# A GRU recurrence with a weight quantiser beside it: pieces of six blocks instead of seven, and the eight blocks left over quantised in chunks 2 to 6 of layer 0

## What is computed

```
h = scan(GRU cell, cond, x)                    # 32 sequential steps, batch 64, width 256
x = x + attention0(h)                          # 16 heads of 128, causal, q and k normalised
x = x + ffn0(conv0(x, cond) + b)               # 8-bit rows, ternary weights, silu(gate) * up, RMS norm
x = x + attention1(cond_block(x, cond))
x = x + ffn1(conv1(x, cond))                   # weights w_fc, w_proj through mse_quant_dequant

def mse_quant_dequant(w):                      # blocks of 64 along the input dimension, int5
    base = max(max|w| in block, 1e-8) / 15
    for s in linspace(0.4, 1.0, 16):           # keep the scale with the least squared error
        deq = clip(round(w / (base * s)), -15, 15) * base * s
        err = sum((deq - w) ** 2)
    return clip(round(w / best), -15, 15) * best
```

## Time and profile before

| | us |
|---|---|
| median of 3 runs | 1393.39 (1392.47 to 1393.52) |
| profiled execution, its own time | 1392.67 |
| its span | 1390.9 |
| busy: PE, DVE, ACT, POOL | 1296.4, 1134.4, 783.6, 134.8 |

### The profile page before, as it was taken

The page is one execution under the profiler, slowest core; times in us unless marked ns, Lnnn a source line. Parts: engine busy times, 40 slices in busy tenths (PEclk is TensorE's granted clock), DMA queues, the critical chain, the costliest instruction groups (busy, mean ns, idle before and its releaser), DMA issues.

```text
span 1390.9 us, 25071 instructions
## 1 busy us (share of the span) xinstructions
PE 1296.4 (93%) x9490; PEld 928.4 (67%) x9490; DVE 1134.4 (82%) x2903; ACT 783.6 (56%) x1486; POOL 134.8 (10%) x152
## 2 busy tenths in 40 slices
PE   5999999999999999999999848898999999999988
PEld 2444444578778787888877535576777778686867
DVE  4799999789988678686969799578788888878775
ACT  3999998865546565655555544534353534445213
POOL 0000000101020101011011100000111111110100
PEclk9999999999999999999999979898999999999999
DMA  9332332531111120202122310000000000000000
GB/s 380 115 76 65 72 100 64 159 119 35 35 39 47 31 60 19 77 1 77 29 99 82 125 38 1 24 16 16 1 24 1 24 1 24 8 8 9 8 1 23
DMA packets 26533, 74.18 MB, mean 53 GB/s; under 512 B 3992, under 2 KB 5156, under 8 KB 25136
## 3 DMA queue, kind: packets, MB, share of 16 engines
q1 hardware_dynamic: 25840, 71.62, 16.5%
q10 hardware_dynamic: 576, 0.98, 0.2%
HBM read 49.52 MB, written 23.07 MB: 52 GB/s over the span
## 4 chain that ended last, share of the span: by engine, by line
PE 65%; DVE 28%; ACT 4%; issue 2%; DMA 1%; SPq 0%; DVEq 0%; ACTq 0%
PE psum L616 14%; PE psum L966 8%; PE psum L725 7%; PE psum L937 7%; DVE ffn_mem L1944 4%; DVE work L1827 4%; PE psum L664 4%; PE psum L980 3%; DVE work L1958 3%; PE psum L1005 3%; PE psum L629 2%; PE psum L883 2%; PE psum L674 2%; PE psum L960 1%; PE psum L650 1%
## 5 line engine op out<-in xcount | busy, mean ns | idle before, releaser
L616 PE MATMUL psum<-h_all,w_big 128*128 128x256 f32 x1024 | 242.5, 385 | 1.0 <-ACT work L1269 1.0
L616 PEld LDWEIGHTS psum<-h_all,w_big 128*128 128x128 f32 x1024 | 189.0, 191 | 41.1 <-issue 15.3
L1827 DVE SCALAR_TENSOR_TENSOR work<-work,taps 128x248 f32<-128x248 f32 (+30 forms) x558 | 149.5, 347 | 0.0
L570 PE MATMUL psum<-w_big,h_all 128*64 128x512 f32 x512 | 124.2, 607 | 0.0
L937 PE MATMUL psum<-work,w_big 128*128 128x256 f32 x512 | 119.8, 381 | 0.5 <-DVE gru_mem L2377 0.5
L725 PE MATMUL psum<-w_big,gru_mem 128*128 128x256 f32 x512 | 113.6, 379 | 0.5 <-ACT gru_mem L1311 0.5
L966 PE MATMUL psum<-w_big 128*128 128x256 f32 x448 | 107.3, 391 | 0.0
L725 PEld LDWEIGHTS psum<-w_big,gru_mem 128*128 128x128 f32 x512 | 96.9, 190 | 14.7 <-ACT gru_mem L1311 0.6
L937 PEld LDWEIGHTS psum<-work,w_big 128*128 128x128 f32 x512 | 95.5, 190 | 15.7 <-DVE gru_mem L2377 3.3
L966 PEld LDWEIGHTS psum<-w_big 128*128 128x128 f32 x448 | 85.1, 194 | 19.5 <-issue 7.7
L2375 DVE TENSOR_TENSOR gru_mem<-psum,trig 128x256 f32<-128x256 f32 x128 | 53.8, 420 | 44.2 <-PE psum L937 41.2
(11 more groups left out here) (325 smaller groups left out, 2578.5 us busy)
## 6 DMA issues: line engine op xcount, KB each, us to landing
value_rows<-w_emb SPq DMA_DIRECT2D x128, 128.0 KB, 2.3
work<-value_rows SPq DMA_DIRECT2D x16, 1024.0 KB, 5.8
w_big<-in_Wq SPq DMA_DIRECT2D x2, 2048.0 KB, 16.6
w_big<-in_Wo SPq DMA_DIRECT2D x2, 2048.0 KB, 20.9
out<-w_big SPq DMA_DIRECT2D x15, 256.0 KB, 2.0
x_res<-out SPq DMA_DIRECT2D x15, 256.0 KB, 2.7
w_big<-in_Wv SPq DMA_DIRECT2D x1, 2048.0 KB, 17.4
w_big<-in_Wk SPq DMA_DIRECT2D x1, 2048.0 KB, 23.1
```

The lines of the kernel that those rows point to most:

```text
L570: mm = pe.matmul(bank(4 + n)[j * B:(j + 1) * B, :], h_all[:, k, :, 2 * pair + j], w_big[:, 2, k * H * HD + n * 512:k * H * HD + (n + 1) * ...
L616: mm = pe.matmul(bank(n % 2)[:, o * TA:(o + 1) * TA], w_big[:, s, k * H * HD + at:k * H * HD + at + HD], h_all[:, k, bass.ds(i * BA, BA), ...
L1827: ins = dve.scalar_tensor_tensor(dst[:, :, lag:], src[:, :, :T - lag], tap, dst[:, :, lag:], ALU.mult, ALU.add)
```

## The change

The pieces shrink from seven blocks to six: `PB = 6`, `PC` = 384 columns, still eight pieces and 32 groups. 16 blocks are then left over, in two halves of `RB = 8`. The first half is the `rest` of before, in its place. The second half, `last` (512 columns from `LAST_AT`), isn't loaded at the start but after chunk 0, into the part of `w_emb` from which PE takes the last piece in layer 1, so that it is neither stored nor loaded again. Its search runs on DVE: `last_begin` (chunk 2) and `last_errors` (chunks 3 to 6) stand between the row maximum and the wait for POOL's root in `quantise_hidden(c - 1, 0)`; `last_group` (chunks 2 to 5) and `last_out` (chunk 6) stand at the end of the chunk, behind `quantise_y`. `last_out` is `rest_out` on `last`, with the product by the scale, which POOL makes for the rest, on DVE at its end. ACT squares (`last_squares`, chunks 3 to 6) behind `hidden_squares(c - 1, 0)`. SP waits in the last chunk for the last sum before it loads W_qkv, and PE waits for the end of `last_out` before it turns the weights.

```diff
-PB = 7
+PB = 6
-RB = NBLK - PIECES * PB
+RB = (NBLK - PIECES * PB) // 2
+LAST_AT = REST_AT + RC
+        last = w_emb[:, 2 * D:2 * D + RC]
+        last_abs = w_big[:, 2, 2560:2560 + RC]
+        last_tmp = w_big[:, 2, 0:GROUP * RC].rearrange("p (j n) -> p j n", j=GROUP)
@@ sync
-            sp.dma_start(w5[:, PC:], io["w5"][:, PC:]).then_inc(w5_in, 16)
+            sp.dma_start(w5[:, PC:LAST_AT], io["w5"][:, PC:LAST_AT]).then_inc(w5_in, 16)
             def last_chunk(i):
+                sp.wait_ge(rest_sum.sem, 2 * NG)
-                for n in range(PIECES):
+                for n in range(PIECES - 1):
                     sp.dma_start(w5_back[n], w5_dram[:, n * 512:(n + 1) * 512]).then_inc(w5_again, 16)
             chunk(0, False, False)
+            sp.wait_ge(film_sum.sem, 1)
+            sp.dma_start(last, io["w5"][:, LAST_AT:]).then_inc(w5_in, 16)
             chunk(1, False, True)
@@ tensor
-                    pe.wait_ge(w5_again, 16 * PIECES)
+                    pe.wait_ge(w5_again, 16 * (PIECES - 1))
+                    pe.wait_ge(rest_done.sem, 2)
@@ scalar
+            def last_squares(n):
+                act.wait_ge(rest_set.sem, NG + n + 2)
+                rest_sq.raised_by(act.activation(last_tmp, last_tmp, ACT.Square))
                 if tail:
                     hidden_squares(c - 1, 0)
+                    if i > 2:
+                        last_squares(i - 3)
@@ vector
+            def last_begin():
+                dve.wait_ge(w5_in, 32)
+                link(dve.tensor_reduce(rest_amax, blocks(last), AX.X, ALU.max, apply_absolute_value=True))
+                link(dve.tensor_scalar(rest_base, rest_amax, 1e-8, None, ALU.max))
+                link(dve.tensor_scalar(rest_base, rest_base, 1.0 / QMAX, None, ALU.mult))
+                link(dve.reciprocal(rest_inv, rest_base))
+                link(dve.tensor_tensor(blocks(last), blocks(last), per_block(rest_inv), ALU.mult))
+                link(dve.scalar_tensor_tensor(last_abs, last, -1.0, last, ALU.mult, ALU.max))
+            def last_group(g):
+                if g:
+                    dve.wait_ge(rest_sum.sem, NG + g)
+                for j in range(GROUP):
+                    ins = dve.tensor_scalar(last_tmp[:, j, :], last_abs, float(1.0 / SHRINKS[g * GROUP + j]), MAGIC,
+                                            ALU.mult, ALU.add)
+                link(ins)
+                link(dve.tensor_scalar(last_tmp, last_tmp, MAGIC + QMAX, MAGIC, ALU.min, ALU.subtract))
+                for j in range(GROUP):
+                    ins = dve.scalar_tensor_tensor(last_tmp[:, j, :], last_abs, -float(1.0 / SHRINKS[g * GROUP + j]),
+                                                   last_tmp[:, j, :], ALU.mult, ALU.add)
+                rest_set.raised_by(ins)
+            def last_errors(g):
+                dve.wait_ge(rest_sq.sem, NG + g + 1)
+                rest_sum.raised_by(dve.tensor_reduce(rest_err[:, g * GROUP:(g + 1) * GROUP, :].rearrange("p s b -> p (s b)"),
+                                                     blocks(last_tmp.rearrange("p j n -> p (j n)")), AX.X, ALU.add))
...
-            def quantise_hidden(c, g, flink):
+            def quantise_hidden(c, g, flink, meanwhile=None):
                 flink(dve.tensor_reduce(h_max, hid_w, AX.X, ALU.max, apply_absolute_value=True))
+                if meanwhile:
+                    meanwhile()
                 dve.wait_ge(hr_on.sem, GA * c + g + 1)
-                    quantise_hidden(c - 1, 0, tail_link)
+                    quantise_hidden(c - 1, 0, tail_link, lambda: last_errors(i - 3) if i > 2 else last_begin())
                     hidden(c - 1, 1, (0,))
+                if tail:
+                    if i - 2 < NG:
+                        last_group(i - 2)
+                    else:
+                        last_out()
```

More of the change, by code:

```diff
@@ L494, in _ @@
             chunk(0, False, False)
+            sp.wait_ge(film_sum.sem, 1)
+            sp.dma_start(last, io["w5"][:, LAST_AT:]).then_inc(w5_in, 16)
             chunk(1, False, True)
             sp.wait_ge(rest_done.sem, 1)
-            sp.dma_start(w5_dram[:, REST_AT:], rest).then_inc(w5_out, 16)
-            with sp.Fori(0, NA - 3) as last:
-                chunk(last + 2, True, True)
+            sp.dma_start(w5_dram[:, REST_AT:LAST_AT], rest).then_inc(w5_out, 16)
+            with sp.Fori(0, NA - 3) as later:
+                chunk(later + 2, True, True)
             last_chunk(NA - 1)
@@ L1717, in _ @@
             pool.wait_ge(in_step.sem, in_step.at(PIECES + 1, 0))
-            rest_based.raised_by(pool.tensor_tensor(blocks(rest), blocks(w5[:, REST_AT:]), per_block(rest_inv), ALU.mult))
+            rest_based.raised_by(pool.tensor_tensor(blocks(rest), blocks(w5[:, REST_AT:LAST_AT]), per_block(rest_inv), ALU.mult))
             times_scale(PIECES - 2)
@@ L1782, in _ @@
             rest_done.raised_by(pool.tensor_tensor(blocks(rest), blocks(rest), per_block(rest_scale), ALU.mult))
-            with pool.Fori(0, NA - 3) as last:
-                chunk(last + 2, True, True)
+            with pool.Fori(0, NA - 3) as later:
+                chunk(later + 2, True, True)
             head_rms(UNITS - 2)
@@ L1895, in slink @@
                     link(ins, in_step, PIECES)
-                slink(dve.tensor_reduce(rest_amax, blocks(w5[:, REST_AT:]), AX.X, ALU.max, apply_absolute_value=True))
+                slink(dve.tensor_reduce(rest_amax, blocks(w5[:, REST_AT:LAST_AT]), AX.X, ALU.max, apply_absolute_value=True))
                 slink(dve.tensor_scalar(rest_base, rest_amax, 1e-8, None, ALU.max))
@@ new lines, in last_errors, with last_out @@
+            def last_errors(g):
+                dve.wait_ge(rest_sq.sem, NG + g + 1)
+                rest_sum.raised_by(dve.tensor_reduce(rest_err[:, g * GROUP:(g + 1) * GROUP, :].rearrange("p s b -> p (s b)"),
+                                                     blocks(last_tmp.rearrange("p j n -> p (j n)")), AX.X, ALU.add))
+            def last_out():
+                dve.wait_ge(rest_sum.sem, 2 * NG)
+                link(dve.tensor_tensor(rest_err, rest_err, shrinks_sq.unsqueeze(2).broadcast_to([P, NS, RB]), ALU.mult))
+                link(dve.tensor_reduce(rest_best, rest_err.rearrange("p s b -> p b s"), AX.X, ALU.min))
+                link(dve.tensor_tensor(rest_pick, rest_err, rest_best.unsqueeze(1).broadcast_to([P, NS, RB]), ALU.is_gt))
+                link(dve.scalar_tensor_tensor(rest_pick, rest_pick, 2.0, shrinks.unsqueeze(2).broadcast_to([P, NS, RB]),
+                                              ALU.mult, ALU.add))
+                link(dve.tensor_reduce(rest_shr, rest_pick.rearrange("p s b -> p b s"), AX.X, ALU.min))
+                link(dve.reciprocal(rest_ishr, rest_shr))
+                link(dve.tensor_tensor(rest_scale, rest_shr, rest_base, ALU.mult))
+                link(dve.tensor_tensor(blocks(last), blocks(last), per_block(rest_ishr), ALU.mult))
+                link(dve.tensor_scalar(last, last, float(QMAX), -float(QMAX), ALU.min, ALU.max))
+                link(dve.tensor_scalar(last, last, MAGIC, MAGIC, ALU.add, ALU.subtract))
+                rest_done.raised_by(dve.tensor_tensor(blocks(last), blocks(last), per_block(rest_scale), ALU.mult))
```

## The result

| | before | after |
|---|---|---|
| median of 4 runs, us | 1393.45 | 1377.07 |
| lowest and highest | 1392.47 to 1393.73 | 1375.23 to 1377.25 |
| profiled execution, its own time | 1392.67 | 1376.97 |
| its span | 1390.9 | 1375.2 |
| busy: PE, DVE, ACT, POOL | 1296.4, 1134.4, 783.6, 134.8 | 1296.0, 1147.1, 775.0, 134.2 |

The changed kernel takes 0.988 of the time (0.986 to 0.990). It is 16.4 us faster in the medians and 15.7 in the spans of the two traces. DVE works 12.7 us more in all and PE the same. The change pays although it adds work: it takes work from where DVE is in the chain and puts more of it where DVE is not.

A forecast was written before the change was run, and what follows sets the result against it. DVE was taken to bound the recurrence and PE layer 0, with PE setting most recurrence steps after the change. Terms -16.3 - 0.3 + 1.6 = -15.0 us gave 1377.7 profiled, 1378.4 us as median (1374.4 to 1382.5).

The forecast's parts named there:

- The recurrence: Last 28 steps: PE's pitch of 6.95 us sets 26 steps, 7.03 and 6.76 the others; 16.3 us saved.
- Rival (a): Recurrence: DVE still sets the steps, at about 6.86 us; 18.7 us saved, kernel 1376.0; chance 0.15.
- The start: Early load: 256 KB less before the constants land saves at most 0.7 us; 0.3 taken.
- After the recurrence: End of the recurrence: DVE ends its quantiser tail sooner but waits for PE's value tiles; nothing gained.
- the stall: Hidden quantiser, chunks 2 to 6: added DVE work delays the third hidden product and so PE; 1.6 us lost.
- the slack of 0.30: Chunks 2 to 6: third hidden product ends at 533.60, PE wants it for its weights at 533.93; 0.30 us spare.
- less what the load overlaps: Chunks 3 to 6: PE's delay of about 0.4 us each, reduced by the load's overlap to 0.34.
- The group fits: End of chunks: a group's 5.22 us fits into 5.69 us of DVE idleness with 0.47 to spare; costs nothing.
- rival (b): Chunks: thinner cover, DVE delays paid whole (3.6 us), groups overrun by 0.4 x 4; 1382.0 us; chance 0.13.
- Rival (d): Chunks: the added 37.3 us of DVE work is not hidden; paid whole 1414.1 us, slower; chance 0.04.
- The rule against it: Chunk 2: two-input DVE products would wait for POOL's power, 1.3 us once; left out of the sum.

The follow-up runs named there:

- the kernel with the work in the chunks alone: Kernel before (seven blocks a piece) plus the last eight blocks' load and search in chunks 2 to 6, done twice: median 1397.76 us, ratio 1.003.
- the doubled group: Changed kernel with each group of four at the end of chunks 2 to 5 computed twice: 1401.09 us, 1.007 of before.

## Why the prediction was right, point by point

1377.07 us against a forecast of 1378.4 (1374.4 to 1382.5), faster as expected. The mechanism is the forecast's; of its terms, some were off in size.

**The recurrence: right, -16.07 for -16.3.** PE's pitch was taken from the single step that PE had set in the kernel before, 6.95 us; 26 steps run at 6.94 to 6.97. Half of the small miss is step 30, 7.16 us for 7.03, the other half the 0.006 by which the 26 steps exceed 6.95; step 31 had 6.75 for 6.76. The prices per column held to 3 ns. Rival (a) was nearer than its 0.15 suggests: DVE stands 0.09 us behind PE.

**The start: the term was mis-sized, -1.19 for -0.3, and for another reason.** The constants land 0.62 us earlier, near the 0.7 that was the bound. DVE timelines of the instruction that waits for them, before and after:

```profile
21.55 0.21 DVE L1993 TENSOR_SCALAR cols<-cols 128x1 f32<-128x1 f32 x1 [4.46 <-DMA shrink_tab<-in_shrinks]
```

```profile
20.93 0.21 DVE L2049 TENSOR_SCALAR cols<-cols 128x1 f32<-128x1 f32 x1 [3.60 <-DMA shrink_tab<-in_shrinks]
```

But the transposition of step 1 starts at 24.01 us instead of 24.19, 0.18 earlier. In the chain after, ACT's scalings of the first group come last there, and no longer the landing:

```profile
18.55 2.14 ACT work L1210 x4
```

In the second trace of the changed kernel this transposition starts at 24.34, so the 0.3 of the forecast can't be told from scatter. The other microsecond of the first pair lies in step 2, and is the clock. Windows of 8 us over step 2: before, after, and the kernel with the work in the chunks alone, whose early load is before's:

```profile
24.00:32.00 8.00, 7.33 (x24) 2.69 (x26) 6.83 (x18) 4.25 (x8) 0.94 (x1) 0.60 1.01 428
```

```profile
23.80:31.80 8.00, 7.30 (x30) 2.86 (x30) 6.63 (x19) 3.93 (x8) 0.83 (x1) 0.79 1.00 426
```

```profile
24.00:32.00 8.00, 6.63 (x26) 2.58 (x28) 6.92 (x19) 4.68 (x9) 0.94 (x1) 0.79 1.02 432
```

At a clock of 0.60 the step, from one transposition to the next, is 9.3 us long, at 0.79 it is 8.3 and 8.1. The third kernel has the early load of before and the clock of after, so the smaller load is not the cause. What else is, stays open; both traces of the kernel before have the long step 2 (9.3 us), all others 8.0 to 8.3.

**After the recurrence: 0 forecast, -0.46 measured.** The argument that DVE's tail brings nothing held. Not seen was that PE's wait for step 31's state shrinks from 2.15 to 1.48 us. Behind the longer one, part of the next 24 products ran at the lower clock (6.94 us for 24; at the 3.72 for 16 of the kernel after it would be 5.58). Windows of 4 us behind it, before and after:

```profile
252.00:256.00 4.00, 4.00 (x12) 2.71 (x9) 2.72 (x6) 4.00 (x7) 0.00 (x0) 0.57 0.50 115
```

```profile
235.00:239.00 4.00, 4.00 (x18) 2.96 (x16) 2.75 (x6) 4.00 (x8) 0.00 (x0) 1.00 0.44 101
```

PE gains 1.4 us there and then waits 0.97 more for ACT's copies, so 0.46 is left. It repeats: both traces of before have 142.77 us in this stretch, the second of after 142.31.

**Chunks 2 to 6: right in place, the stall mis-sized, +0.60 for +1.6.** Timelines of the changed kernel: DVE, PE and PE's weight loads (PEld) in chunk 4, then DVE at the end of chunk 2 (columns as in the earlier trace rows):

```profile
511.62 2.29 DVE L1979 TENSOR_REDUCE v<-w_big 128x32 f32<-128x2048 f32 x1 [0.58 <-ACT w_big L1285]
513.82 0.20 DVE L2189 TENSOR_SCALAR stats<-stats 128x1 f32<-128x1 f32 x1
...
516.03 0.74 DVE L2169 SCALAR_TENSOR_TENSOR gru_mem<-psum,stats,work 128x512 f32<-128x512 f32 x1
...
516.29 1.14 PE L681 MATMUL psum<-ffn_mem,work 128*128 128x512 bf16 x4
...
516.83 0.11 PEld L681 LDWEIGHTS psum<-ffn_mem,work 128*128 128x128 bf16 x2 [0.43 <-DVE gru_mem L2169]
...
531.58 0.73 DVE L1837 TENSOR_SCALAR work<-work,taps,cols 128x256 f32<-128x256 f32 x2 [0.54 <-ACT work L1348]
```

```profile
433.73 1.43 DVE L1968 TENSOR_SCALAR w_big<-w_big 128x512 f32<-128x512 f32 x4
435.19 1.23 DVE L1971 TENSOR_SCALAR w_big<-w_big 128x2048 f32<-128x2048 f32 x1
436.45 2.50 DVE L1973 SCALAR_TENSOR_TENSOR w_big<-w_big 128x512 f32<-128x512 f32 x4
439.51 0.75 DVE L2169 SCALAR_TENSOR_TENSOR gru_mem<-psum,stats,work 128x512 f32<-128x512 f32 x1 [0.56 <-ACT work L1331]
```

The reduction of the squared differences waits 0.58 us for ACT, as said, and what follows is 0.60 late, where the forecast had 0.74: DVE's next instruction starts, at 513.82, before the row of the reduction ends (511.62 + 2.29), and I had added up ends. PE's group of four takes 1.14 us instead of 1.03: 0.11 a chunk, not 0.34. In the kernel before, the four weight loads of this group follow each other without a wait:

```profile
533.49 0.75 PEld L674 LDWEIGHTS psum<-ffn_mem,work 128*128 128x128 bf16 x4
```

In the changed kernel the third, which belongs to the first up product, starts 0.32 us late. So the slack of 0.30 held: 0.60 - 0.32 = 0.28. Two terms of the stall were mis-sized. The delay was 0.60, not 0.74. And "less what the load overlaps" took off 0.10 (0.44 to 0.34), where the load starts 0.21 ahead of its product and so hides 0.21: 0.32 - 0.21 = 0.11. DVE's wait of 1.01 for ACT's copy of x1 is down to 0.54, so the rest of the delay is taken up there, as said. Chunk 2 lost 0.20, as forecast. The group fits, with 0.56 us left of a forecast 0.47; rival (b) is refuted. Rival (d) had a real mechanism, as the doubled group shows, but here the cover is there. Once it is used up, the work is paid in full and more: 24 us for 20.8 added.

**The transition to layer 1: not foreseen, +1.40.** It is the scatter of this stretch told above, and luck as far as the sum goes. The forecast's sum was -15.0 and the trace has -15.7, but the errors of the terms were -0.9 (start), +0.2, -0.5, -1.0 (stall) and +1.4: they partly cancel, and the sum is closer than its terms. What repeats in both pairs of traces is -16.07, -0.46 and +0.60, together -15.9.

**The rule against it.** In chunk 2 DVE has two-input products beside POOL's powers. Timelines of the changed kernel, DVE and POOL:

```profile
376.66 5.43 POOL L1740 TENSOR_TENSOR stats<-stats,minus_half 128x32 f32<-128x32 f32 x1 [0.49 <-ACT stats L1299]
382.06 0.98 POOL L1744 TENSOR_TENSOR stats<-stats,minus_half 128x1 f32<-128x1 f32 x1
...
378.05 1.23 DVE L2177 TENSOR_TENSOR gru_mem<-gru_mem,ffn_mem 128x1024 f32<-128x1024 f32 x1
...
381.94 0.69 DVE L1961 TENSOR_TENSOR w_emb<-w_emb,stats 128x512 f32<-128x512 f32 x1
```

With these products moved away (the experiment with `last_begin` and `last_errors` behind the third product) POOL's small power took 0.55 us:

```profile
382.59 0.55 POOL L1744 TENSOR_TENSOR stats<-stats,minus_half 128x1 f32<-128x1 f32 x1
```

The Trainium skill ("SBUF — State Buffer", section "Who interferes with whom") has a DVE instruction with two SBUF inputs and a GpSimd one that reads SBUF contend for a shared pair of ports, one excluding the other. DVE's product of 1.23 us lies within POOL's 5.43 and is not longer than with POOL idle (1.22 to 1.23), so on that side the trace does not agree. POOL's small power beside the products took 0.98 for 0.55 us, so on POOL's side something of the kind shows, 0.43 us once (0.98 again in the second trace; such times on POOL are rough). It kept nobody waiting: the second of DVE's products ended later.

## What to carry to other kernels

Where two engines are nearly balanced, find the one step in the trace that the other engine already sets: its start-to-start time is the floor that shortening the first can reach, here to 0.02 us. A stretch is the place for extra work when the engine idles ahead of an instruction whose input comes from elsewhere; add up the work against that idle time, and price an overrun above its length, since PE's wait also costs clock behind it. Before one explains a microsecond at the edges of a trace, one should run the same kernel twice.

## What the runs showed of the hardware

The granted clock of one stretch differs between executions of one program: 166.01 and 163.30 us for the same instructions. The Trainium skill ("TensorE: Matmul & The Clock Gate", Part 1) says that the number of slow products at a kernel's start varies from run to run; here it is seen in the middle too. The two traces of the changed kernel differ by 2.4 us in their spans and by 2.7 in this stretch.

Four waits of 3.66 us on PE were followed by 7 to 11 products at the lower level. The wait of 1.48 us for the state of step 31 in the changed kernel was followed by none, the one of 2.15 us in the kernel before by a granted clock of 0.57 in 252 to 256 us. The length of the wait alone doesn't tell: with fewer value products and five blocks a wait of 1.10 us at this place was followed by a clock of 0.57 in 226 to 230 us, where PE had idled 0.48 us in each step before, and with five blocks alone 0.79 us by a full clock.
